# A routed two-layer kernel: first table moves on another queue, indices made earlier, empty steps of the second routing at other places

## The reference, cut to what matters

```
x = x + attn_a(layernorm(x))        # 1024 x 1024 mixing matrix, the same for all heads
x = x + ffn(layernorm(x), gate_w, w1, w2)
x = x + attn_b(layernorm(x), w_q, w_k, w_v, w_o)
x = x + ffn(layernorm(x), gate_w, w1, w2)

def ffn(x, gate_w, w1, w2):         # 8 experts, 256 tokens each per sequence
    probs = softmax(einsum('ntd,ed->nte', x, gate_w))
    g, m = top_k(probs.transpose(0, 2, 1), 256)       # each expert picks its tokens
    h = gelu(einsum('nekd,edf->nekf', x[batch_idx, m], w1))
    h = einsum('nekf,efd->nekd', h, w2)
    return zeros.at[batch_idx, m].add(g[..., None] * h)
```

## Time and profile before

| | |
|---|---|
| median of 3 runs | 2235.77 us (2234.77 to 2235.8) |
| profiled execution, its own time | 2237.5 us |
| its span | 2235.8 us |
| busy share of the span | PE 96%, weight loads 71%, DVE 66%, POOL 61%, ACT 45% |
| granted TensorE clock, mean | 0.987 |

### The profile page before, as it was taken

How to read it: one execution, slowest core, us unless ns; L and a number is a source line. 1 busy time by engine, 2 the same in 40 slices (tenths; PEclk the granted TensorE clock), 3 DMA queues, 4 the chain that set the end, 5 groups by cost and what they waited for, 6 DMA issues and landing times.

```text
span 2235.8 us, 34077 instructions
## 1 busy us (share of the span) xinstructions
PE 2149.9 (96%) x12130; PEld 1597.8 (71%) x12130; DVE 1465.4 (66%) x3349; ACT 1003.6 (45%) x1907; POOL 1368.7 (61%) x1237
## 2 busy tenths in 40 slices
PE   6998999999999999999999999999999899999997
PEld 5455788889876666766657666667666588889997
DVE  6365688675757666467674577874877636975553
ACT  4411553444445545345553354542554425434443
POOL 2322676677537776566674576664677846777774
PEclk9899999999999999999999999999999999999999
DMA  4432544555432212212312222221220244545552
GB/s 132 144 129 86 151 117 111 151 144 137 114 88 67 51 36 76 67 52 73 76 48 67 67 78 56 58 61 54 76 76 21 76 132 115 140 113 139 134 144 29
DMA packets 145048, 206.04 MB, mean 92 GB/s; under 512 B 19432, under 2 KB 112112, under 8 KB 144880
## 3 DMA queue, kind: packets, MB, share of 16 engines
q1 hardware_dynamic: 120304, 170.30, 25.4%
q0 software_dynamic: 24576, 33.57, 8.8%
HBM read 130.03 MB, written 39.85 MB: 76 GB/s over the span
## 4 chain that ended last, share of the span: by engine, by line
PE 73%; DVE 9%; issue 4%; POOL 4%; ACT 2%; DMA 1%; SPq 1%; POOLq 0%; DVEq 0%; ACTq 0%
PE psum L1299 12%; PE psum L1320 11%; PE psum L1446 11%; PE psum L1348 7%; PE psum L1411 7%; PE psum L1427 6%; PE psum L1471 5%; PE psum L1362 4%; PE psum L1376 3%; PE psum L1456 3%; POOL t_acc L2390 2%; DVE f_hlo L2134 1%; DVE f_hhi L2132 1%; PE psum L1389 1%; PE psum L1267 1%
## 5 line engine op out<-in xcount | busy, mean ns | idle before, releaser
L1713 ACT ACTIVATE t_p<-psum 128x512 f32<-128x512 f32 (+3 forms) x768 | 323.6, 492 | 294.3 <-PE psum L1427 284.6
L2390 POOL TENSOR_TENSOR t_acc<-t_acc,t_p 128x1024 f32<-128x1024 f32 (+3 forms) x256 | 416.9, 1629 | 14.5 <-ACT t_p L1713 0.5
L2309 POOL TENSOR_TENSOR f_wlo<-f_wst,f_whi 128x256 fp32r<-128x256 f32 x256 | 221.8, 922 | 150.6 <-ACT f_whi L1646 150.6
L1320 PE MATMUL psum<-f_whi,f_hhi 128*128 128x256 f32 x1024 | 294.9, 288 | 6.2 <-DVE f_hlo L2134 6.1
L1446 PE MATMUL psum<-t_p,t_v 128*64 128x512 f32 (+3 forms) x1536 | 288.8, 496 | 7.3 <-POOL t_p L2370 7.3
L1320 PE MATMUL psum<-f_whi,f_hlo 128*128 128x256 f32 x1024 | 289.4, 283 | 0.0
L1320 PE MATMUL psum<-f_wlo,f_hhi 128*128 128x256 f32 x1024 | 289.2, 282 | 0.0
L2132 DVE CAST f_hhi<-f_h 128x512 fp32r<-128x512 f32 x256 | 141.9, 554 | 208.0 <-ACT f_h L1664 153.2
L1664 ACT ACTIVATE f_h<-psum 128x512 f32<-128x512 f32 x256 | 153.0, 598 | 275.8 <-PE psum L1299 246.8
L1411 PE MATMUL psum<-t_qa,t_ka 128*128 128x512 f32 (+3 forms) x768 | 222.7, 370 | 1.8 <-DVE t_mx L2180 0.6
L2390 POOL TENSOR_TENSOR t_acc<-t_p 128x768 f32<-128x768 f32 x64 | 134.6, 2103 | 136.4 <-PE psum L1456 133.1
(11 more groups left out here) (288 smaller groups left out, 4408.1 us busy)
## 6 DMA issues: line engine op xcount, KB each, us to landing
f_wst<-in_L_ffn_w SPq DMA_DIRECT2D x64, 1024.0 KB
t_ka<-t_ka SPq DMA_DIRECT2D x64, 256.0 KB, 3.3
t_qb<-t_qa SPq DMA_DIRECT2D x64, 256.0 KB, 4.0
t_wk<-wkT SPq DMA_DIRECT2D x32, 256.0 KB, 4.0
t_wq<-wqT SPq DMA_DIRECT2D x32, 256.0 KB, 4.0
t_wv<-wvT SPq DMA_DIRECT2D x16, 512.0 KB, 4.9
normal<-f_xy SPq DMA_DIRECT2D x5, 1024.0 KB, 10.3
a_x<-in_L_attn_a_x SPq DMA_DIRECT2D x4, 1024.0 KB, 10.0
```

The costliest lines, as they stand in the source:

```text
L1320: m = pe.matmul(out, h[:, js], w[:, f, :], start=(f == 0 and a == 0 and j % 2 == 0), stop=(f == FT - 1 and a == 2), skip_group_check=True)
L1713: act.activation(p[:, i, q0:], k.bank[bank][:, q0:], ACT.Exp, scale=1.0 / float(np.sqrt(k.DH))).then_inc(k.drained[bank], 1)
L2309: m = pool.tensor_tensor(t["wlo"][n % 2][:, i, ks], t["wst"][:, i, ks], t["whi"][n % 2][:, i, ks].bitcast(F32), ALU.subtract)
L2390: pool.tensor_tensor(acc[:, :, q0:], (p0 if kt == 1 else acc)[:, :, q0:], p[:, :, q0:], ALU.add).then_inc(k.p_acc, 1)
```

## The change

1. For r = 0 alone the sixteen table DMAs go from SyncE's queue to ScalarE's (new `table_move` in ScalarE; SyncE's returns at once).
2. For every r, `indices` of the first table is made before `table_move` of the second. The order of marks on VectorE's semaphore follows this.
3. For r = 0 the second `indices` waits (in the order of the program, not on the chip) until `mix_residual(1, 6)` has been issued; that is the flag `mixed`. For r = 0 there are three instead of one empty steps between the second `table` and the first `indices`.
4. For r = 1 the routing begins after one empty step instead of four, has five instead of three empty steps behind the softmax sum, and one more between `compare` and `rank`. The first layer norm is so issued three steps earlier, the threshold search one step earlier, everything from `rank` on at the same step.

```
-        for i in range(k.NBLK - 2, k.NBLK):
-            self.mix_residual(1, i)
+        self.mix_residual(1, k.NBLK - 2)
+        self.mixed = True
+        yield
+        self.mix_residual(1, k.NBLK - 1)
...
         self.softmax_sum(r, t)
-        yield
-        yield
-        yield
+        for _ in range(5 if r == 1 else 3):
+            yield
...
         self.compare(r, t)
         yield
+        if r == 1:
+            yield
         self.rank(r, t)
...
         self.table_move(r, 0, pair[0], t)
         self.table(r, 1, t)
-        yield from steps(1, 3)
+        yield from steps(3, 3)
+        self.indices(r, 0, pair[0], t)
         self.table_move(r, 1, pair[1], t)
         yield
-        for i, b in enumerate(pair):
-            self.indices(r, i, b, t)
+        while r == 0 and not self.mixed:
+            yield
+        self.indices(r, 1, pair[1], t)
...
         if r == 1:
-            for _ in range(4):
-                yield
+            yield
         for i in range(2):
             self.route_load(r, i, pair[i], t)
...
+    def table_move(self, r, i, b, t):          # ScalarE
+        k, act = self.k, self.e
+        if r:
+            return
+        self.wait_ge(k.d_route.sem, k.d_route.at(r, ("R", i)))
+        for e in range(k.E):
+            act.dma_start(t["tab"][b][:, e].rearrange("q h t -> q (h t)"),
+                          t["R"][i][16 * e:16 * (e + 1), :]).then_inc(k.q_tab[i], DMA)
...
     def table_move(self, r, i, b, t):          # SyncE
+        if r == 0:
+            return
```

More of the change, by code:

```diff
@@ L110, in semaphores @@
                              "key", "hi4", "lo4",
-                             *[(step, i) for i in range(2) for step in ("A", "hot", "C0", "C1")], ("R", 0), ("R", 1),
-                             ("idx", 0), ("row", 0), ("idx", 1), ("row", 1))
+                             *[(step, i) for i in range(2) for step in ("A", "hot", "C0", "C1")], ("R", 0), ("idx", 0),
+                             ("row", 0), ("R", 1), ("idx", 1), ("row", 1))
         self.pe_mixed = s("pe_mixed_gate")
@@ L682, in stage_f @@
         self.norm_of, self.routed, self.loaded, self.through = {}, -1, 0, 0
-        self.turned = 0
+        self.turned, self.mixed = 0, False
         first, second = iter(()) if layer else self.route(0), self.route(2 * layer + 1)
@@ L927, in route @@
             yield from [None] * 2
+            self.indices(2, 0, 0, early)
             self.table_move(2, 1, 1, early)
@@ L930, in route @@
                 yield
-            for b in range(2):
-                self.indices(2, b, b, early)
+            self.indices(2, 1, 1, early)
             self.routed = 2
```

## The result

| | before | after |
|---|---|---|
| median, 5 runs each | 2235.8 us | 2244.03 us |
| lowest to highest | 2234.77 to 2238.76 | 2242.5 to 2249.0 |
| profiled execution, its own time | 2237.5 us | 2242.5 us |
| its span | 2235.8 us | 2240.7 us |
| granted TensorE clock, mean | 0.987 | 0.988 |

The ratio of the times is 1.0045, 95% interval [1.0034, 1.0056]: slower by 8.2 us in the medians (by the interval of the ratio, 7.6 to 12.5 us), where 8.55 was forecast. The profiled execution is the fastest of its five runs; its span is only 4.9 us longer.

A forecast was written before the change was run, and what follows sets the result against it. TensorE, busy 96% of the span, was taken as the bound, so its waits and lower clock count. 0.9 + 4.1 - 0.85 + 4.4 = +8.55 us on 2235.77 gave 2244.3; 8-in-10 range 2235.0 to 2250.5.

The forecast's parts named there:

- term 1: First routing: tables start 0.8 us earlier on ScalarE's queue, but second indices come 1.6 late; +0.9 us.
- term 2: Units 0 to 2, norm three steps earlier: new waits 2.1 and 5.0, clock 1.4, old losses -4.4; +4.1 us.
- term 3: Threshold search one step earlier: the 1.35 us wait at `compare` goes, +0.5 for other waits; -0.85 us.
- term 4: Routings 1 to 3, second reduction behind first indices: 1.5 + 1.7 (lower clock) in routing 1, 1.2 in routing 3; +4.4 us.
- A: Rival: new waits in units 0 to 2 don't reach PE, term 2 is -4.4; 2235.9 us, no change; chance 0.22.
- B: Rival: issuing from ScalarE is cheap, second table isn't delayed, term 1 is -4.5; 2238.9 us; chance 0.08.
- C: Rival: row load lands by 217.5, VectorE has no stall, table waits are partly covered; faster, 2230.5 us; chance 0.10.

The follow-up runs named there:

- e1: Kernel before with only the first routing's sixteen table DMAs moved to ScalarE's queue; 2234.2 us against 2234.62, ratio 0.9999.
- e8: Kernel before with routing 0's table DMAs half on ScalarE's, half on SyncE's queue, plus change item 3's residual order; 2239.12 us against 2240.7, ratio 0.9992.
- e7: Kernel before with change item 4 alone, but two empty steps at the start and four behind the softmax sum; 2244.68 us against 2240.7, ratio 1.0014.
- e10: Kernel before with change item 4 alone, and routing 1's row loads behind the first `up` product instead of the third; 2242.65 us, ratio 1.0015.
- e11: e10 with the second block's norm at its old step, so only the first block's is three steps earlier; 2235.34 us against 2234.46 before, ratio 1.0004.
- e2: Kernel before with only the first table's indices ahead of the second reduction, in every routing, tables on SyncE's queue; 2239.69 us, ratio 1.0023.
- e9: e8 with routing 1's threshold search one step earlier, as in e5; 2232.86 us against 2234.46 for the kernel before, ratio 0.9992.
- e5: Kernel before with only routing 1's threshold search one step earlier, first layer norm at its old step; 2240.31 us against 2240.7, ratio 1.0002.
- e4: Kernel before with change items 1 and 3: first routing's tables on ScalarE's queue, residual block ahead of the second indices; 2235.24 us, ratio 1.0003.

## Why the prediction was right

**First routing (term 1, +0.9).** Right: 21.83 us to the first `up` where six executions of the old order have 20.3 to 20.85 (mean 20.66): +1.2, or +1.0 against before alone, and its two pieces are the forecast ones: second indices 1.67 us later (1.6), rows 0.69 sooner behind them (0.7). The price of an issue on ScalarE's queue, taken from SyncE's, held (0.65 against 0.64 us, e1).

The Trainium skill ("DMA: Bandwidth & Descriptors", Issuing engines are not separate DMA queues) calls the time that issuing from several engines saves usually small relative to the DMA. The trace differs on that here too: halving the issues of each queue brought some 2 us (e8).

**Units 0 to 2 (term 2, +4.1).** The sum is near, 4.24, its pieces are not. Forecast were new waits of 2.1 and 5.0, 1.4 for the clock and 4.4 of old ones gone. The old ones went. Found were 3.07 in unit 0, 1.7 for the clock behind it (0.57 over 4 us), 2.12 + 1.23 in unit 1, and a new 0.95 at the second block's `f_wide` (282.06). The step that failed is "PE is there at 248.5. PE loses 5.0". The end of that wait was right: the GELU was to be ready at 253.5 and was at 253.4 (253.72 + 0.59, less the 0.89 by which the frame of after is late). PE's arrival was taken from the trace of before, though PE had lost 3.57 us by the third `up` of unit 1, and 2.1 by the prediction's own count; it came at 251.35 (254.36 - 2.12 - 0.89). So PE lost 2.12 and not 5.0: a loss in the first place shortens the wait in the second, as e7 and e10 show (3.53 and 3.61 in unit 1 where unit 0 costs less).

That the sum is near is luck. The double count of 2.9 us was offset by unit 0's longer wait (VectorE took 1.53 us for a weight split instead of 1.22 and 2.08 and 1.65 for two pairs of casts instead of 1.12, each beside a split on GpSimd, and `f_rstd` took 2.59 instead of 1.7), by the 1.23 and by the 0.95. And of the 2.05 us counted as gone, 1.1 belonged to the slow product in the one trace of before; against the traces without it the term is 5.4.

It also named the load's wait as the start of the chain. That was true of unit 0, but without it 4.9 of the 6.1 us are still lost up to unit 2 (e10). The second norm's turn on ScalarE decides (e11).

**Threshold search (term 3, -0.85).** Small as said, and smaller: -0.30 in the changed kernel, ratio 1.0002 alone. The wait for `f_ge` went, but the +0.5 for its replacements was too little: they cost 1.05.

**Routings 1 to 3 (term 4, +4.4).** The waits are right: 2.32 us at unit 7 (2.2 to 2.8 forecast) and 1.60 in routing 3 (1.4). The shifts are 1.29 and 1.41 for the forecast 1.5 and 1.2. The 1.7 us for a lower clock didn't come in this execution, and did in e2.

**The sum.** 0.9 + 4.2 - 0.3 + 1.3 + 1.4 = 7.5 in the traces, plus 1.1 if most executions of before lack the slow product of its trace, so 8.6, against 8.2 in the medians. That 8.55 had been forecast is luck in part: term 2 was 1.3 too small and term 3 0.55, term 4 was 1.7 too large. That the two spans differ by only 4.9 is the attention, in which nothing was changed: -2.47 us there between these two executions, and between +0.1 and -3.1 against before in the other eleven. TensorE's timeline of the changed kernel at two places that look alike, and the windows behind them:

```profile
1141.80 0.70 PE L1431 MATMUL psum<-t_qb,t_kb 65*128 65x512 f32 x2 [2.23 <-DMA t_qb<-t_neg]
...
1441.22 1.19 PE L1431 MATMUL psum<-t_qb,t_kb 65*128 65x512 f32 x2 [2.21 <-DMA t_qb<-t_neg]
```

```profile
1142.00:1144.00 2.00, 2.00 (x11) 1.74 (x11) 1.92 (x4) 1.64 (x4) 0.59 (x2) 1.00 0.86 219
...
1442.00:1444.00 2.00, 2.00 (x7) 1.81 (x7) 1.88 (x6) 1.92 (x5) 0.41 (x1) 0.50 0.57 162
```

The same wait was followed by full clock at the first place and by half at the second. In before both were followed by half clock.

**Rivals.** A (the waits don't reach PE) fell with the 3.07 and 2.12 us; B with e1; C with the load's 2.33 us wait, and e10, which gave it that load earlier, was still slower than the kernel before.

**Left open.** Why the first `up` product of unit 2 is signalled 1.8 to 2.1 us late in some executions of the same code, most of them on one chip. Whether the second norm's place alone, with the loads at theirs, would bring back all but unit 0's share. And what decides whether 2.2 us of idleness lower the clock.

## What to carry to other kernels

Side work that ends in a wait costs by what stands behind it in that engine's list, not by how early it was begun. Before moving it earlier, follow each of its steps to the engine that does it: if one stands behind a fixed block of other work (here eight indirect DMAs), the result came no sooner (249.0 to 249.2 us in e10, e7 and before), and its consumer waits ahead of work that it used to stand behind. When several waits hang on one chain, add their losses from the end of the chain backwards, not each against the old arrival. And where two transfers are to overlap, keep the second's producer ahead of the wait for the first.

## What the runs showed of the hardware

- Idle times of TensorE of nearly one length are followed by half clock or not, from execution to execution: half behind 2.16 (e2, unit 7), 2.21, 2.22 and 2.23 us; full behind 2.23 and 2.32 us (changed kernel).
- An earlier start after the long wait at the change to the experts is partly given back: half clock for 5.7 and 5.9 us when the first `up` came 2.4 and 2.7 us earlier (e8, e9), 3.7 to 5.3 where it came within 0.8 us of before, 3.0 where it came later (e2, changed kernel).
- TensorE can signal a product late without a gap in its records: from the start of the first `up` of unit 2 to its GELU it is 3.4 to 3.8 us in before, e5, e8 and e7, and 1.7 in e1, e2, e4, e9 and e11.
- A small DMA costs its issuing queue the same on ScalarE as on SyncE (0.65 and 0.64 us from one issue to the next), and two queues issue side by side: 5.2 us instead of 6.4 or more to the second indices.
